# Delta-rule attention with a mixture of experts: three products leave TensorE, two are reordered

## What is computed

```
beta = sigmoid(x @ Wb)                                   # 4 heads
k = k * rsqrt(sum(k * k) + 1e-12)
S_t = S_{t-1} + k_t (beta_t * (v_t - k_t^T S_{t-1}))^T ; o_t = q_t^T S_t
o = o * rsqrt(mean(o * o, axis=-1) + EPS) * norm_w       # mean over the 32 of a head
o = o * (g * sigmoid(g))
x = layernorm(x + o @ Wo)
x = layernorm(x + moe(x))                                # top 2 of 8 experts, with a capacity
```

## Time and profile before

| | us |
|---|---|
| median of 3 runs (lowest to highest) | 535.98 (535.22 to 536.87) |
| the profiled execution | 539.49 |
| its span, first to last instruction | 537.7 |
| PE busy of the span | 490.4 (91%) |
| DVE, ACT, POOL busy | 330.7, 332.4, 319.7 |
| first z_32 product of chunk 0 | at 37.3 |
| first product of the experts (L956) | at 331.3 |

### The profile page before, as it was taken

One profiled execution on the slowest core, in us unless ns is written; L12 is line 12 of the kernel. 1 busy time (PEld: TensorE's weight loads), 2 busy tenths in 40 slices (PEclk: granted clock), 3 DMA queues, 4 the chain that ended last, 5 costly groups with the idle time before them and its releaser, 6 DMA issues.

```text
span 537.7 us, 18954 instructions
## 1 busy us (share of the span) xinstructions
PE 490.4 (91%) x7096; PEld 408.4 (76%) x7096; DVE 330.7 (61%) x1316; ACT 332.4 (62%) x916; POOL 319.7 (59%) x441
## 2 busy tenths in 40 slices
PE   6989999999999999999979977999999999999900
PEld 4666767767777777776656667999999999999900
DVE  4436567767687676876955872565455654555344
ACT  3646777777777877777743642554555545555456
POOL 3053528757578575785883452376677766767650
PEclk9999999999999999999985998999999999999975
DMA  3358753762545725436383234254555545553366
GB/s 93 31 86 226 257 112 44 107 93 31 66 46 59 102 33 72 49 46 99 34 166 39 27 33 109 36 109 55 108 107 76 109 55 108 93 85 36 31 135 204
DMA packets 136820, 45.83 MB, mean 85 GB/s; under 512 B 89568, under 2 KB 131296, under 8 KB 136736
## 3 DMA queue, kind: packets, MB, share of 16 engines
q1 hardware_dynamic: 114864, 29.60, 27.0%
q0 software_dynamic: 20288, 9.51, 19.4%
q10 hardware_dynamic: 1584, 5.59, 2.6%
HBM read 21.13 MB, written 23.55 MB: 83 GB/s over the span
## 4 chain that ended last, share of the span: by engine, by line
PE 71%; DMA 9%; POOL 7%; issue 5%; SPq 3%; ACT 2%; DVE 1%; POOLq 1%; ACTq 0%; DVEq 0%
PE ps L956 19%; PE ps L970 13%; PE ps L694 4%; PE ps L679 4%; POOL slots_in L1665 3%; PE ps L650 3%; PE ps L653 3%; PE ps L654 2%; PE ps L655 2%; POOL xs L1648 2%; PE ps L914 2%; PE ps L718 2%; POOL prod L1647 2%; DMA a_diag<-hb 1%; PE ps L728 1%
## 5 line engine op out<-in xcount | busy, mean ns | idle before, releaser
L1706 POOL DMA_INDIRECT x_store<-xk,row x80 | 123.9, 1549 | 68.5 <-ACT xk L1214 45.8
L1665 POOL DMA_INDIRECT slots_in<-x,slot x64 | 98.7, 1542 | 25.6 <-issue 17.3
L1540 DVE TENSOR_TENSOR hb<-ps,hs 128x320 f32<-128x320 f32 (+1 forms) x128 | 62.7, 491 | 53.1 <-ACT hs L1206 52.6
L1206 ACT ACTIVATE hs<-ps 128x320 f32<-128x320 f32 (+1 forms) x128 | 55.7, 435 | 34.5 <-PE ps L956 33.5
L970 PE MATMUL ps<-w2s,hb 128*128 128x128 f32 x640 | 74.1, 275 | 0.0
L970 PEld LDWEIGHTS ps<-w2s,hb 128*128 128x128 f32 x640 | 72.8, 192 | 0.0
L956 PE MATMUL ps<-xeTh,w13h 128*128 128x320 f32 x224 | 71.3, 318 | 0.9 <-DVE xeTl L1564 0.9
L956 PE MATMUL ps<-xeTl,w13h 128*128 128x320 f32 x224 | 69.9, 312 | 0.0
L956 PE MATMUL ps<-xeTh,w13l 128*128 128x320 f32 x224 | 69.9, 312 | 0.0
L1214 ACT ACTIVATE xk<-ps,gs 128x128 f32<-128x128 f32 x80 | 24.1, 364 | 45.4 <-PE ps L970 45.4
L1647 POOL TENSOR_TENSOR prod<-a,xs 128x28 f32<-128x28 f32 (+11 forms) x120 | 32.5, 271 | 25.5 <-DVE xs L1375 16.7
(11 more groups left out here) (210 smaller groups left out, 1085.3 us busy)
## 6 DMA issues: line engine op xcount, KB each, us to landing
slots_in<-zeros ACTq DMA_DIRECT2D x10, 520.0 KB, 5.0
xe<-slots_in SPq DMA_DIRECT2D x15, 325.0 KB, 2.9
w<-w_in SPq DMA_DIRECT2D x8, 448.0 KB, 4.0
xTs<-xT SPq DMA_DIRECT2D x4, 512.0 KB, 5.1
a_diag<-hb SPq DMA_DIRECT2D x64, 32.0 KB, 1.9
inv<-xs SPq DMA_DIRECT2D x16, 128.0 KB, 2.7
xi<-inv SPq DMA_DIRECT2D x16, 128.0 KB
xk<-x SPq DMA_DIRECT2D x8, 256.0 KB, 4.0
```

Source lines behind the costliest of these rows:

```text
L1206: af(hs[to, s % 4, :], ps[src, HB[fill_of(s) % 5], 0:HALF], ACT.Silu).then_inc(hs_ready, 1)
L1540: v.tensor_tensor(hb[rows_, par, c, HALF * g:HALF * g + HALF], ps[rows_, at, 0:HALF], hs[rows_, s % 4, :], ALU.mult).then_inc(h_ready, 1)
L1665: g.indirect_dma_start(out=xs_d[:, :], out_offset=bass.IndirectOffsetOnAxis(ap=to, axis=0), in_=x1[:, p % 2, j, k, :], in_offset=None, com ...
L1706: g.indirect_dma_start(out=x1_d[:, :], in_=ye[:, par, i, :], in_offset=None, out_offset=bass.IndirectOffsetOnAxis(ap=row[:, par, i:i + 1], ...
```

## The change

Four things change.

1. `values` makes values and denominators in one product of 132 columns for each sequence. The denominators come out as 128 tokens by 4 heads instead of 4 by 256, so their product of its own, its split weights `wbs`, and two copies that made them go. `eb` is 128 partitions by 8, the DRAM tensor is stored token by unit, and the load of `denb` becomes a strided one of single elements. `scale_blocks` waits for a semaphore of each parity.
2. `project_x` multiplies by the router's 8 columns alone. DVE adds x in f32 (`normalise`, new tile `x0`), and statistics and rows are taken from `x0`. `project_x` waits for `top_out` in place of `x1_ready`.
3. `head_sums` becomes two F32R products, of the squares' high part `osqh` and low part `osql`. ACT writes the square twice, DVE subtracts (`squares_low`).
4. In PE's list `key_key` goes ahead of `z_128`, and `head_sums` goes behind `state_keys`. In ACT's list `key_key_out` goes ahead of `z128_copy`.

The diff, cut to its core:

```diff
-    bd_d = nc.dram_tensor("den_store", (2, U, P), F32, kind="Internal").ap()
+    bd_d = nc.dram_tensor("den_store", (2, P, U), F32, kind="Internal").ap()
...
-        eb = sb("eb", [H, 2, 2 * P])
+        eb = sb("eb", [P, 2, B, H])
...
             def send_blocks(n):
                 sp.wait_ge(den_out, n + 1)
-                wait(sp, den_ld, 16 * (n - 1))
-                sp.dma_start(bd_d[n % 2].rearrange("(b h) t -> h b t", b=B),
-                             eb[:, n % 2].rearrange("h (b t) -> h b t", b=B)).then_inc(den_st, 16)
+                wait(sp, den_ld[n % 2], 16 * (n // 2))
+                sp.dma_start(bd_d[n % 2], eb[:, n % 2].rearrange("p b h -> p (b h)")).then_inc(den_st, 16)
...
-                sp.dma_start(denb[half], bd_d[n % 2].rearrange("u (k r) -> (u k) r", r=16)).then_inc(den_ld, 16)
+                sp.dma_start(denb[half].unsqueeze(2), bd_d[n % 2].rearrange("(k r) u -> u k r", r=16).unsqueeze(3),
+                             allow_slow_non_contiguous=True).then_inc(den_ld[n % 2], 16)
...
             def values(n):
                 to = free_bank("v", n)
                 for b in range(B):
-                    mm(ps[:, to, P * b:P * b + P], xTs[:, b, cols(n)], wvb[:, 0:H * DV], start=True, stop=True)
-                products(ps[0:H, to, 256:512].rearrange("p (b t) -> p b t", b=B), wvb[:, H * DV:VW], wbs,
-                         n).then_inc(fill_mm, 1)
+                    last = mm(ps[:, to, VW * b:VW * b + VW], xTs[:, b, cols(n)], wvb[:], start=True, stop=True)
+                last.then_inc(fill_mm, 1)
...
             def head_sums(p):
                 pe.wait_ge(o_out, p + 1)
-                mm(ps[:, OB, 256:512], heads[:], osq[:], start=True, stop=True).then_inc(sum_mm, 1)
+                pe.wait_ge(osql_out, p + 1)
+                mm(ps[:, OB, 256:512], headsr[:], osqh[:], start=True, stop=False)
+                mm(ps[:, OB, 256:512], headsr[:], osql[:], start=False, stop=True).then_inc(sum_mm, 1)
...
-                    pe.wait_ge(x1_ready, p)
+                    pe.wait_ge(top_out, p)
...
-                    mm(ps[:, MB, XW * b:XW * b + XW], xTs[:, b, cols(p)], rx[:], start=(b == 0), stop=False,
+                    mm(ps[:, MB, XW * b + D:XW * b + XW], xTs[:, b, cols(p)], rx[:, D:XW], start=(b == 0), stop=False,
                        skip_group_check=True)
...
-                at(head_sums, p - 5)
                 at(state_keys, p - 4)
+                at(head_sums, p - 5)
...
-                af(osq[:], ps[:, OB, 0:2 * P], ACT.Square)
+                af(osqh[:], ps[:, OB, 0:2 * P], ACT.Square)
+                af(osq[:], ps[:, OB, 0:2 * P], ACT.Square).then_inc(osq_out, 1)
                 af(o[:], ps[:, OB, 0:2 * P], ACT.Copy).then_inc(o_out, 1)
...
+            def squares_low(p):
+                dve.wait_ge(osq_out, p + 1)
+                v.tensor_tensor(osql[:], osq[:], osqh[:].bitcast(F32), ALU.subtract).then_inc(osql_out, 1)
...
                 dve.wait_ge(proj_mm, p + 1)
+                dve.wait_ge(xk_ld[p * 2 // NP], 16 * B)
+                link(v.tensor_tensor(x0[:], ps[:, MB, 0:2 * XW].rearrange("p (j c) -> p j c", j=2)[:, :, 0:D],
+                                     xk[:, :, p, :], ALU.add))
...
-                    last = v.tensor_scalar(x1[:, p % 2, j, :, 0:D], bc(rows_of(j), 1, TOPK), mv[:, j, 0:1],
+                    last = v.tensor_scalar(x1[:, p % 2, j, :, 0:D], bc(x0[:, j, :], 1, TOPK), mv[:, j, 0:1],
                                            rstd[:, j:j + 1], ALU.subtract, ALU.mult)
...
                 at(state_copy, p - 6)
+                at(squares_low, p - 6)
                 at(masked, p - 5, 0)
```

More of the change, by code:

```diff
@@ L268, in build @@
         osq = sb("osq", [P, 2 * P])
+        osqh = sb("osqh", [P, 2 * P], F32R)
+        osql = sb("osql", [P, 2 * P], F32R)
+        headsr = sb("headsr", [P, P], F32R)
         osl = sb("osl", [P, 2 * P])
@@ L277, in build @@
         rstd = sb("rstd", [P, 2])
+        x0 = sb("x0", [P, B, D])
         x1 = sb("x1", [P, 2, B, TOPK, W])
@@ L312, in build @@
         wgs = [w_[:, 2 * H * D:2 * H * D + H * DV] for w_ in wide]
-        wbs = [w_[:, 2 * H * D + H * DV:2 * H * D + H * DV + H] for w_ in wide]
         xhs, xls = (x_[:].rearrange("p a c -> p (a c)").rearrange("p (r b t) -> p r b t", r=XR, b=B)
@@ L367, in build @@
         den_st = sem("den_st")
-        den_ld = sem("den_ld")
+        den_ld = [sem("den_ld0"), sem("den_ld1")]
         a_st = sem("a_st")
@@ L411, in build @@
         o_out = sem("o_out")
+        osq_out = sem("osq_out")
+        osql_out = sem("osql_out")
         sum_mm = sem("sum_mm")
@@ L876, in _ @@
                 at(turn_keys, p - 5)
+                at(key_key, p - 1, 0)
                 at(z_128, p - 5)
-                at(key_key, p - 1, 0)
                 at(project, p - 6)
@@ L905, in _ @@
                 at(z_64, p - 4)
+                at(state_keys, p - 4)
                 at(head_sums, p - 5)
-                at(state_keys, p - 4)
                 at(keys, p, 1)
@@ L1013, in values_out @@
                 wait(act, den_st, 16 * (n - 1))
-                af(eb[:, n % 2], ps[0:H, src, 256:512], ACT.Exp, scale=-1.0).then_inc(den_out, 1)
+                both = ps[:, src, 0:B * VW].rearrange("p (b c) -> p b c", b=B)
+                af(eb[:, n % 2], both[:, :, H * DV:VW], ACT.Exp, scale=-1.0).then_inc(den_out, 1)
                 wait(act, vk_out, n - VR + 1)
-                af(V[:, n % VR], ps[:, src, 0:256].rearrange("p (b c) -> p b c", b=B), ACT.Copy).then_inc(v_out, 1)
+                af(V[:, n % VR], both[:, :, 0:H * DV], ACT.Copy).then_inc(v_out, 1)
             def key_key_out(n, b):
@@ L1138, in weights_high @@
                 af(Mks[0], Mk[:], ACT.Copy)
-                af(wbs[0], wvb[:, H * DV:VW], ACT.Copy)
                 af(wgs[0], wg[:], ACT.Copy)
@@ L1145, in _ @@
             for p in range(NP + LAST):
+                at(key_key_out, p - 3, 0)
                 at(z128_copy, p - 7)
-                at(key_key_out, p - 3, 0)
                 at(t128_copy, p - 7)
@@ L1280, in _ @@
                 v.tensor_scalar(spare_y[:, k // CT, k % CT:k % CT + 1], pcol[:], float(NT * P + P * k), None, ALU.add)
+            v.tensor_copy(headsr[:], heads[:])
             v.tensor_copy(tri[:], upper[:])
@@ L1363, in scale_blocks @@
                 n, r = chunks_in(q)[-1], rows_in(q)
-                dve.wait_ge(den_ld, 16 * n + 16)
+                for m in chunks_in(q):
+                    dve.wait_ge(den_ld[m % 2], 16 * (m // 2) + 16)
                 link(v.tensor_scalar(denp[r], denb[r], 1.0, None, ALU.add))
@@ L1403, in gated_out @@
                 v.tensor_tensor(og[:], osl[:], orms[:], ALU.mult).then_inc(og_out, 1)
-            def rows_of(b):
-                return ps[:, MB, XW * b:XW * b + D]
             def normalise(p):
                 dve.wait_ge(proj_mm, p + 1)
+                dve.wait_ge(xk_ld[p * 2 // NP], 16 * B)
+                link(v.tensor_tensor(x0[:], ps[:, MB, 0:2 * XW].rearrange("p (j c) -> p j c", j=2)[:, :, 0:D],
+                                     xk[:, :, p, :], ALU.add))
                 for j in range(2):
-                    stats = link.mark(v.bn_stats(bst[:, j, :], rows_of(j)))
+                    stats = link.mark(v.bn_stats(bst[:, j, :], x0[:, j, :]))
                 logits = link.mark(v.tensor_copy(lg[:], ps[:, MB, 0:2 * XW].rearrange("p (j c) -> p j c", j=2)[:, :, D:XW]))
@@ L1489, in weights_low @@
                 dve.wait_ge(split_act, 1)
-                for parts, whole in ((Mks, Mk[:]), (wbs, wvb[:, H * DV:VW]), (wgs, wg[:]), (Nqs, Nq[:])):
+                for parts, whole in ((Mks, Mk[:]), (wgs, wg[:]), (Nqs, Nq[:])):
                     last = v.tensor_tensor(parts[1], whole, parts[0].bitcast(F32), ALU.subtract)
```

## The result

| | kernel before | changed kernel |
|---|---|---|
| median of 22 runs each (lowest to highest) | 537.64 (533.32 to 541.34) | 536.95 (529.49 to 543.96) |
| ratio, 95% interval | | 0.9938 (0.9915 to 0.9961) |
| profiled execution, its span | 539.49, 537.7 | 536.93, 535.2 |
| chunk 2's z_32 | 73.27 | 77.38 |
| chunk 2 to chunk 12 | 173.05 | 169.65 |

What follows compares the result with a forecast made beforehand. The prediction took TensorE (PE) to bound the scan's steps: ten steps -7.6, chunks 14 to 15 -0.8, filling +0.5, together -7.9, giving 531.6 for the profiled execution and 528.1 for the median; range 524.0 to 533.8.

Steps and rivals of the forecast that it cites:

- The likeliest case: Whole kernel: TensorE bounds the scan and its shorter list saves 7.9, median 528.1; chance 0.59.
- a step's 0.76: Steady scan step: values 0.42, head sums 0.41 and x 0.05 saved, less 0.12 given back by ACT.
- The head sums' 0.41: Steady step, z_64 to keys: two F32R products behind state_keys without a tile-size change save 0.41.
- The values' 0.42: Steady step, values to turn_keys: four records of 132 columns replace seven, 0.90 becoming 0.48, saving 0.42.
- x's 0.05: Steady step, project_x: four weight loads still cost 0.43, so dropping 128 of 136 columns saves only 0.05.
- The rule of 25 ns between small products: project_x by the skill's rule: four products would take 0.10, and ten steps would save 3.8 more.
- ACT's 0.12: Steady step: later head_sums delay ACT's norms and keys' copy, so values wait; 0.12 given back each step.
- The end, -0.8: Behind chunk 12: nothing saved to chunk 14, 0.8 saved from 14 to 15, then PE's 0.4 cancels DVE's 0.4.
- one fall that comes earlier: Rival, scan's end: more PE idling drops the clock at chunk 12, 13 more, total 541; chance 0.10.
- not at all, at 0.05: Rival, between chunks 14 and 15: the clock does not fall, 7.4 less, total 520.7; chance 0.05.
- the inverse's path: Rival, steady steps: scaling, solve and transfers become the bound, 5.5 come back, total 533.6; chance 0.12.
- The filling: Rival, pipeline start: denb's strided load delays three first turns, 4.5 in place of 0.5, total 532.1; chance 0.08.

Runs made afterwards that it cites:

- e3: The changed kernel with ACT's copy of the first half of the keys ahead of the head norms; ratio to the kernel before 0.9912.
- e14: Repeat on another chip of the changed kernel with the keys' copy ahead of the head norms; ratio to the kernel before 0.9972.
- e7: The kernel before with only the head sums' part (two F32R products behind state_keys, second square, squares_low); ratio to the kernel before 0.9978.
- e9: The changed kernel, unaltered, timed again on a second chip; ratio to the kernel before 0.9922.
- e16: The changed kernel, unaltered, timed as control on a third chip; ratio to the kernel before 0.9961.
- e5: The kernel before, unchanged, profiled again in one run; chunk 2 to 12 took 178.79, against 173.05 in its first profile.
- e17: The kernel before with only the x part (project_x multiplies the router's 8 columns, DVE adds x); ratio to the kernel before 1.0081.
- e6: The kernel before with the values' part plus key_key ahead of z_128 and key_key_out ahead of z128_copy; ratio to the kernel before 0.9950.
- e4: The kernel before with only the values' part (one product of 132 columns, strided denb load); ratio to the kernel before 1.0008.
- e2: The kernel before with 14 instead of 22 filler products ahead of chunk 0's z_32; ratio to the kernel before 1.0071.
- e8: The changed kernel with 30 instead of 22 starting fillers and the keys' copy ahead of the head norms; ratio to the kernel before 1.0007.
- e10: The changed kernel with filler products at the scan's end, ahead of chunk 14's z_32 and in the last chunk; ratio to the kernel before 0.9971.

## Why the prediction was wrong

The likeliest case was the right one in its mechanism: TensorE stayed the bound and its shorter list shortened the steps. The step of the prediction that failed is its sum: a step's 0.76 measured 0.5, the last chunk's new operations, which it cancelled to nothing, cost 1.4, and the clock had no term in it. In the two profiled executions the sum of 7.9 became 2.5: the ten steps -3.4 for -7.6, the start +4.1 for +0.5, chunk 12 to the experts -1.8 for -0.8, the experts -1.4 for 0.

1. **The step, 0.76.** It measured 0.52 by its parts and 0.41 to 0.51 by the steps' distances. The head sums' 0.41 was good (0.39). The values' 0.42 was 0.35: four records cost 0.07 more here than those of project_x, which were their price. A change of tile size ahead of them is a likely reason (project's four took 0.46 behind the keys' product and take 0.57 behind z_128's small tiles), but no run isolates it. x's 0.05 was 0.01: the rows were right to let the loads decide. The rule of 25 ns between small products (*TensorE: Matmul & The Clock Gate*, *Back-to-back issue gap* in the Trainium skill) would have given 3.8 in all, and not 3.8 more than the sum's own 0.5 as I wrote; it did not come, since four products of 8 columns take 0.47 here. The same section says that its formula has no budget for loading weights and counts too little for small products, and that is this case. ACT's 0.12 was 0.23, at the very place named, and with the copy first the wait went and the best steps were 16.48 (e3, e14). Ten steps saved 3.4 in place of 7.6; two of them also held stalls of 1.3 together, which wait for nothing shown.
2. **The end, -0.8.** I carried the steps' savings to chunk 15 and took the rest as cancelled. In the last chunk each operation stands in the chain: head sums +0.95 and x +0.45, with the same wait of 0.94 in e7, e9 and e16; another 1.2 stands in its stretches at the low clock. Between chunks 12 and 14 it took 31.5 in place of 30.2; the inverse's two transfers took 3.51 and 3.28 where they had taken 2.43 and 3.10. Other profiles of the change show 30.6 (e9) and 30.0 (e16), so this 1.3 is no property of it. Against all that, chunk 14 to 15 took 16.4 and not 22.2, because the clock was back at 285: that is luck of this execution, 5.8 where I had 0.8.
3. **The clock.** I had it as one fall that comes earlier, at 0.10, or not at all, at 0.05. What happens is in between: short stretches at 1.2 GHz, behind pauses of PE, in places that change from one execution to the next. Every such stretch ahead of the experts has a pause of PE of 0.5 or more before it, but not every pause has such a stretch behind it. One place is regular: in all 10 profiles with the moved sums and no fillers at the end the clock fell in the last chunk, behind the new wait of 0.94, and without the moved sums in 2 of 6 (e5 and e17). Between 0.945 and 0.98 of mean clock one hundredth goes with 3 to 5 us (of the kernel before, 27 and 31 runs on two chips: 3.6 and 3.3 us). Beside the same runs of the kernel before the change has 0.955 against 0.962 (e9) and 0.960 against 0.970 (e16), which would be some 3 us. This is a reckoning from runs beside each other, not an edit that holds the clock and changes nothing else, and it does not add up with the other two: ten steps at 0.41 to 0.51 less the last chunk's 1.4 are already 2.7 to 3.7 (1.2 less with its low stretch), and 3.3 was measured. How much of the missing 4.6 is clock stays open; the steps (2.5 to 3.5) and the last chunk (1.4) cover it without one.

The rivals: the inverse's path did not bind in the steps (no wait ahead of z_32 between chunks 2 and 12 but at chunk 2). The filling did not pay for denb's load: chunk 2 stood at 72.04, 72.35 and 71.71 in e6, e9 and e16, no later than in before. ACT became the bound in part, 0.23 a step. The clock fell at another place than I said, in the filling, as the text's last sentence left open. One reading of the page was off by a slice or two, without effect: PE's nines run from slice 3 to 19, counted from 0.

Shown: what each part is worth in a steady step, that key_key must move with the values (e4, e6), that x alone costs 0.8% (e17, in one group of runs, with the place of the loss unknown), that a pause at the start can cost the clock (e2), that most of a lead ahead of chunk 12 can be lost behind it (e8). Argued only: that the low clock is the cause of the end's losses; from chunk 12 to the experts the time goes loosely with the low time (81.1 at 4 us, 84 to 85 at 17, 89.6 at 27, but also 84.0 at 7 in e6), and the same pauses make both. The change without x was not run, though e6, e7 and e17 point to it.

## What to carry to other kernels

Work taken off the busiest engine is worth its time only in the stretch where nothing else ends last; ask for each stage, the first and last round of a pipeline above all, which of the new operations stands in the open there. Where an engine's clock follows its activity, faster work makes longer pauses and may pay part of the gain back (the change's mean granted clock was lower in both comparisons that show it, e9 and e16), so compare many runs and read the granted clock with the time. One profile of a program whose low stretches move about cannot stand for its median. A product may need its neighbour moved along with it: time the part with and without the reorder.

## What the runs showed of the hardware

- The granted clock can fall to 1.2 GHz behind pauses of 1 to 2 us, and does not always: it did in 5 of 9 profiles in which PE waited 0.4 to 1.7 for chunk 0's inverse and again 0.8 to 1.4 for x (after, e2, e3, e4, e10; not e6, e9, e14, e16), and in none of the 11 in which fillers ran up to z_32. In e9 it fell at 178 behind a single pause of 0.72.
- TensorE can stall for nothing that the profile shows, up to 0.9 at one place in every second step; over ten steps that was 5.7 for the same program (e5 against before). All 14 profiles from three of the chips have such stalls repeatedly in their steps, the 4 from the fourth do not.
- Four products of 128 rows by 8 columns in f32 take 0.47, four with 136 columns 0.48: the columns do not set the pace. Their loads of 128 columns are the same and start 0.11 apart in the earlier trace rows.
